# One item of attention taken out of turn, two MLPs stretched, and separate buffers for the last stage of a four-layer kernel

## The reference, cut to what matters

```python
# L0: RMS norm, 8 query heads of 64 on one key head, rotary; gated MLP 512 -> 2048 -> 512
x = x + softmax(rope(q(h)) @ rope(k(h)).T / 8) @ v(h) @ Wo.T        # h = ada_rms(x)
x = x + (silu(h @ Wg.T) * (h @ Wu.T)) @ Wd.T                        # h = ada_rms(x)
# L1: layer norm, 16 heads of 32, unit-length q and k; MLP with tanh gelu
x = x + (softmax(qn @ kn.T + mask) @ v @ Wproj.T + bproj) * gamma1
x = x + (gelu_tanh(h @ Wfc1.T + bfc1) @ Wfc2.T + bfc2) * gamma2
# L2: layer norm, 16 query heads of 32 on 4 key heads through a latent, banded mask; no MLP
x = x + attention(h) @ Wo.T
# L3: 8 experts, each on its own 64 channels, then a norm and a projection
y = gelu(x_e @ W1_e + b1_e) @ W2_e + b2_e                           # exact gelu
x = x + silu(layernorm(y) * (1 + scale) + shift) @ out_W + out_b
```

## Time and profile before

| what | value |
|---|---|
| median of 3 runs | 2262.67 us (2260.27 to 2266.0) |
| profiled execution, its own time | 2263.43 us |
| its span, first to last instruction | 2261.6 us |
| PE busy in the span | 1991.7 us, 88% |
| DVE, ACT, POOL busy | 1139.3, 1033.9, 795.2 us |
| TensorE clock granted, mean | 0.928 |

### The profile page before, as it was taken

The page is one execution under the profiler, slowest core; times in us unless marked ns, Lnnn a source line. Parts: engine busy times, 40 slices in busy tenths (PEclk is TensorE's granted clock), DMA queues, the critical chain, the costliest instruction groups (busy, mean ns, idle before and its releaser), DMA issues. The chain is left out here.

```text
span 2261.6 us, 35138 instructions
## 1 busy us (share of the span) xinstructions
PE 1991.7 (88%) x12920; PEld 1560.5 (69%) x12920; DVE 1139.3 (50%) x3157; ACT 1033.9 (46%) x2445; POOL 795.2 (35%) x1095
## 2 busy tenths in 40 slices
PE   5698999899999999998999899999889975877675
PEld 3476778687778878886778788778767753635353
DVE  3645444643453455346645655565465454544442
ACT  2423322332343344434554565455365467474744
POOL 4454444111124233334656434243233333322210
PEclk9789989999999999999999999999999997987977
DMA  7225566444444544454445343334433520312100
GB/s 269 80 83 177 180 235 236 152 168 149 163 138 160 197 149 142 148 187 145 155 140 196 130 154 128 131 117 140 141 125 131 192 97 29 103 38 83 39 29 19
DMA packets 93659, 309.58 MB, mean 137 GB/s; under 512 B 10417, under 2 KB 11185, under 8 KB 91825
## 3 DMA queue, kind: packets, MB, share of 16 engines
q1 hardware_dynamic: 93488, 307.34, 39.2%
HBM read 240.19 MB, written 67.11 MB: 136 GB/s over the span
## 5 line engine op out<-in xcount | busy, mean ns | idle before, releaser
L164 POOL TENSOR_SCALAR SS<-SS,NM 128x256 f32<-128x256 f32 (+1 forms) x640 | 290.4, 471 | 909.8 <-DVE NM L179 909.8
L149 PE MATMUL B<-HM,W 128*128 128x512 f32 x2496 | 589.4, 396 | 23.6 <-DVE HM L167 15.1
L149 PEld LDWEIGHTS B<-HM,W 128*128 128x128 f32 x2496 | 475.5, 191 | 125.5 <-issue 22.6
L149 PE MATMUL B<-G,W 128*128 128x512 f32 x1536 | 409.8, 418 | 34.7 <-DVE FB L170 17.7
L149 PEld LDWEIGHTS B<-G,W 128*128 128x128 f32 x1536 | 299.3, 199 | 110.2 <-issue 44.0
L155 ACT ACTIVATE SS<-SS,NM 128x256 f32<-128x256 f32 (+1 forms) x512 | 240.6, 471 | 205.9 <-DVE NM L164 205.1
L152 PE MATMUL B<-ident,SS 128*128 128x128 f32 x1152 | 185.2, 301 | 63.2 <-POOL SS L164 52.8
L149 PE MATMUL B<-HA,W 128*128 128x512 f32 x864 | 227.1, 414 | 6.9 <-DVE HA L167 6.3
L152 PEld LDWEIGHTS B<-ident,SS 128*128 128x128 f32 x1152 | 134.2, 150 | 99.7 <-POOL SS L164 58.3
L149 PEld LDWEIGHTS B<-HA,W 128*128 128x128 f32 x864 | 167.2, 200 | 46.4 <-DVE HA L167 6.7
L167 DVE TENSOR_TENSOR G<-FB,G 128x512 fp32r<-128x512 f32 x128 | 102.2, 799 | 160.7 <-ACT G L155 160.7
(11 more groups left out here) (102 smaller groups left out, 2680.6 us busy)
## 6 DMA issues: line engine op xcount, KB each, us to landing
W<-kept SPq DMA_DIRECT2D x360, 512.0 KB, 4.2
kept<-W SPq DMA_DIRECT2D x120, 512.0 KB, 4.7
ST<-in_wpack SPq DMA_DIRECT2D x120, 256.0 KB, 3.0
Y<-in_adaw SPq DMA_DIRECT2D x12, 1024.0 KB, 6.5
out_xT<-X SPq DMA_DIRECT2D x16, 256.0 KB, 2.0
X<-in_xT SPq DMA_DIRECT2D x1, 3072.0 KB, 14.3
FB<-in_pos SPq DMA_DIRECT2D x4, 256.0 KB, 5.0
X<-in_xT SPq DMA_DIRECT2D x1, 1024.0 KB, 6.0
```

What stands on the lines that cost most here:

```text
L149: return self.real.matmul(*a, **k) if self.real is not None else self
L164: return self.real.tensor_scalar(*a, **k) if self.real is not None else self
```

## The change

It has five parts.

1. **The order of the items** becomes a table. The seventh and eighth places are now (layer 2, chunk 0) and (layer 1, chunk 3): item 7 is layer 2 of chunk 0, item 8 is layer 1 of chunk 3, the rest as before. All formulas on g go through it.
2. **The positions** are now a table of numbers, `PLACE`, with a start and an end of its own for each MLP and single positions for norms, projections, experts and last products.
3. **G has memory of its own**, so that the experts no longer wait for the last MLP. W12 and its DMA are gone: the expert weights are four pieces of 128x512 (256 KB) that go through the two stages ST, one per group t and chunk, unsplit.
4. **z writes its high and low parts into the memory of T and Y** (ZH, ZL) in place of HM. The statistics of the next norm, which use T and Y, therefore wait until the four `last` products of the z before them are done.
5. **WSLOTS 11 to 8, FBUFS 5 to 7.**

```diff
-ITEMS = 12
+ORDER = ((0, 0), (0, 1), (0, 2), (0, 3), (1, 0), (1, 1), (1, 2), (2, 0), (1, 3), (2, 1), (2, 2), (2, 3))
...
-PIECES = 120
-WSLOTS = 11
+PIECES = 124
+WSLOTS = 8
...
-FBUFS = 5
+FBUFS = 7
...
-UPS = (20.4, 38.4, 55.8, 71.8, 87.8, 103.8, 119.8, 135.8, 151.8)
+PLACE = {
+    "up": [20.25, 37.774, 53.238, 69.246, 84.763, 103.509, 123.675, 150.322],
+    "up end": [35.49, 53.408, 66.177, 84.262, 100.64, 123.811, 147.706, 164.324],
+    "m norm": [17.582, 34.064, 49.554, 66.056, 81.912, 97.369, 120.398, 147.186],
+    "m final": [19.93, 36.106, 52.069, 68.347, 84.611, 99.748, 122.714, 149.431],
+    "a norm": [3.951, 20.163, 36.916, 52.263, 68.917, 84.642, 101.558, 116.342, 131.609, 150.183, 166.089],
...
+    "first": [137.43, 168.366, 179.31, 201.305],
+    "z norm": [141.577, 174.923, 183.457, 207.201],
+    "z final": [144.398, 176.596, 185.493, 212.617],
+    "last": [145.545, 178.406, 187.993, 221.687],
...
+    "experts": [0.314, 0.533, 1.113, 0.998],
+    "z stats": [-0.298, 0.784, 0.756, 1.406, 2.27],
+    "z parts": [0.874, 2.977, 1.615, 0.743],
+    "last step": [0.67],
...
+    "down": [0.802],
...
-        self.at(UPS[8] + 0.2, self.add, "w12")
...
-        with nc.sbuf_tensor("G", [128, 4, 2, 512], F32R) as G:
-            pass
+        G = sb("G", [128, 4, 2, 512], F32R)
         GF = sb("GF", [128, 4, 512])
-        W12 = sb("W12", [128, 4, 512])
...
+        with nc.sbuf_tensor("ZL", [128, 4, 512], F32R) as ZL:
+            pass
         Y = sb("Y", [128, 4, 512])
...
+        with nc.sbuf_tensor("ZH", [128, 4, 512], F32R) as ZH:
+            pass
         T = sb("T", [128, 4, 512])
...
+        def stats_read(i):
+
+            return p_last.of(i[2], 3) if i[0] == "z" else p_var.of(i)
...
                     e.wait_ge(*source_ready(i))
-                    e.wait_ge(*p_var.of(norm_before[i]))
+                    e.wait_ge(*stats_read(norm_before[i]))
...
-                    w, x = W12[:, t, :], X[:, t, 512 * n:512 * n + 512]
-                    e.wait_ge(*s_w12.of())
+                    w, x = ST[:, weights.stage(number(n, "experts", 3, t)), :], X[:, t, 512 * n:512 * n + 512]
+                    e.wait_ge(*ready(n, "experts", 3, t))
...
-                    product(dp.buf(u)[:, :], [(part(w, 128 * c, 128 * c + 128), (HM[:, 0, c, :], HM[:, 1, c, :]))
+                    product(dp.buf(u)[:, :], [(part(w, 128 * c, 128 * c + 128), target(("z", 0, n), c))
...
-            return p_second.of(*divmod(i - 1, 4)) if i else p_down.of(7, 3, 3)
+            return p_second.of(*divmod(i - 1, 4)) if i else (None, 0)
...
-                elif kind == "w12":
-                    e.wait_ge(*p_down.of(7, 3, 3))
-                    e.dma_start(W12[:, :, :], w12).then_inc(*s_w12.up())
```

More of the change, by code:

```diff
@@ L186, in halves, with layer, _kept_values @@
     return ap.rearrange("p (b s) -> p b s", b=2)
+def layer(g):
+    return ORDER[g // 16][0]
 def unit(g):
-    return g // 64, (g // 16) % 4, (g // 4) % 4, (g // 2) % 2, g % 2
+    return *ORDER[g // 16], (g // 4) % 4, (g // 2) % 2, g % 2
 def keys(g):
-    return 128 if g // 64 == 2 and g % 2 == 0 else 256
+    return 128 if layer(g) == 2 and g % 2 == 0 else 256
+def _kept_values():
+    first, ends = [], []
+    for k, (L, n) in enumerate(ORDER):
+        first.append(len(ends))
+        ends += [16 * k + 4 * t + 3 for t in range(4)] if L == 1 else [16 * k + 15]
+    return first, ends
+KV_FIRST, KV_END = _kept_values()
 def kv_number(L, n, t):
-    return n if L == 0 else 4 + 4 * n + t if L == 1 else 20 + n
+    return KV_FIRST[ITEM[L, n]] + (t if L == 1 else 0)
 def pair(g):
@@ L334, in unit @@
         if 0 <= g < UNITS:
-            us = [self.dp.take() for _ in range(keys(g) * HEADS[g // 64] // 512)]
+            us = [self.dp.take() for _ in range(keys(g) * HEADS[layer(g)] // 512)]
             self.add("turn", g, us)
@@ L493, in pieces_of @@
         return [("down", q // 4, 4 * c + j) for j in range(4)], q % 4
+    if kind in ("first", "second"):
+        return [("experts", 3, a[1])], a[0]
     if kind == "last":
@@ L577, in spread @@
             need = [self.number[name, n] for name in names]
-            while waiting and not (self.raw(waiting[0])):
+            while waiting and not self.raw(waiting[0]):
                 do(waiting.pop(0))
@@ L583, in spread, with program @@
                 assert x < w and x not in waiting, (step, x, w)
+                while self.plain(x) and self.order[x] >= loaded:
+                    load()
             out.append(step)
+            if step[0] == "second":
+                split += 1
+                load()
             store(lambda y: False)
-            if waiting:
+            if waiting and (not self.raw(waiting[0]) or self.order[waiting[0]] < split + STAGES):
                 do(waiting.pop(0))
         return out
-def program(nc, xT, pos, condT, biasd, cols, consts, tab2, wpack, w12, adaw, out):
+def program(nc, xT, pos, condT, biasd, cols, consts, tab2, wpack, adaw, out):
     ctx = ExitStack()
@@ L1014, in tensor @@
                     r.then_inc(*p_second.up(n, t))
+                    w = number(n, "experts", 3, t)
+                    stused[weights.order[w]] = (p_second, (n, t))
                 elif kind == "last":
```

178 lines of the change are left out of this document (103 added, 75 removed), and 1 row of the table PLACE.

## The result

The changed kernel takes **2168.81 us** (median of 4 runs, 2165.85 to 2172.67) where the kernel before, on the same chip, takes 2261.47 (2259.09 to 2266.0): ratio 0.9589, 95% interval 0.9567 to 0.9611, 93 us less. The forecast was 2230 us, 32 less, with 2192 as the low end. The profiled execution took 2169.68 us.

What follows compares the result with a forecast made beforehand. PE bounds the kernel (busy 1991.7 of 2261.6 us), so reordering wins only its standing and low clock. 2263.4 - 43 + 8 + 3 + 2 - 3 = 2230.4, put at 2230 us; own range 2216 to 2244, with rivals 2192 to 2262.

Steps and rivals of the forecast that it cites:

- The cover: Units 152 to 164: MLP 7 replaces the chunk 0 tail's thin chain there; gain 43 us, ends 39 and 47.
- The 6.6 us: Loss left for the 76.0 us of work of units 152 to 164 once covered, at 8.7%.
- MLP 7's share: Units 152 to 164: some 75 us of MLP put there, 12 of 14 units.
- The gaps: 10.8 units without an MLP, attention alone: 8 us lost at 0.75 a unit, from 0 to 17.
- Eight places: Weight fetches at part starts begin later with 8 places, not 11; few land late: 3 us lost.
- the third rival: Slower: at 32 part starts PE waits for fetches landing in 8 us, 80 us for 3; 2307 us, chance 0.12.
- z in T and Y: After chunk 0's tail, MLP 7's norm wants T before the last product is done; 2 us lost, once.
- The start: Before unit 20: slices called a thin start; no term for it in the sum.
- The spacing of the tails: Tails of chunks 1 to 3: z statistics further apart, later z norm in chunk 1; 3 us gained, from 0 to 27.
- None is on the path: 0 us: Chunk 0 tail's new place: twelve more ACT table loads, 15 us of ACT, priced at 0 us.
- The rival of more: Last 300 us: half the T and gelu waits freed, 19 us, 27 with the clock; 2204 us, chance 0.20.

## Why the prediction was right in direction and wrong in size

**The cover, 43 us: right in the sum, not place by place.** Unit 152 to 164 takes 120.8 us (forecast 120 to 130) with PE at 98% and a clock of 0.99. The stretch lost 49.6 us and loses 120.8 - 117.6 = 3.2. Unit 152 comes 57.5 us earlier, of which 17.3 lie before unit 20 and 40.2 behind it, where the forecast had 40. But the tail of chunk 0 now lies in units 136 to 151, and these lose 27.5 us where they lost 4.1 in the kernel before; units 128 to 135 lose 1.0 for 18.2. With the natural order units 136 to 151 lose 133.6 - 0.92 x 119.0 = 24.1 us with no tail in them, so the 27.5 aren't the tail's alone. The 6.6 us that the prediction left for the covered work can be read off no stretch. Nor can the term be read off one experiment, since undoing the stretch of MLPs 5 and 6 keeps MLP 7's and gives 18 us. (MLP 7's share in that paragraph, 12 of 14 units, is 80 us and not 75; the sum doesn't use it.)

**The gaps, +8 us: wrong in sign.** Closing three of the gaps makes the kernel 24 us slower. The step that failed was to take two rows of the end of layer 2, and "lost a unit" from them, for what attention alone would do behind an MLP of layers 0 and 1. It charged the gap for itself and nothing for the parts, the norm and the output product that crowd together without it. Which of these it is, no run shows.

**Eight places, +3 us: about right here, by the wrong wait.** At the old positions they cost some 12 us in units 16 to 79, 9.9 of them in PE's waits for POOL's split of a new piece; at the new ones eight against nine cost nothing visible. No fetch is waited for, so the third rival (2307 us) is out, and its 8 us of landing never came up: the median is 4.3.

**z in T and Y, +2 us.** It wasn't tried by itself. The wait where it was put is small: in units 136 to 151 of the changed kernel PE stands for T 4.9 us in two waits, with and without cover much the same.

The stretch from 20 to 163 is 45.0 us shorter, not 30. That is 15 of the 61 us missed.

**The start, no term: 17 us.** The step that failed is the list of what moves: it had the MLPs, the tails and the buffers, and treated the new positions of the first item (q, k, v, norm, trig) as nothing, after calling the start thin. The earlier trace rows had the sign of it, PE at 5 and 6 tenths and then the clock at 7. The runs put 12 us of it on the positions (7 on the value product alone) and 5 to 6 on the smaller pool.

**The spacing of the tails, -3 us: 31.6, with 29 back in one run.** This is the step that failed by most. The prediction had the wait (27.2 us for T) and even its full size as an end, and then took a tenth of it. It also had the rival: half of the waits for T and gelu, 19 us, with the clock that comes back, 27 us. The size and the place are that rival's, the make-up only in part: T and gelu fell by 13 us, and the waits for PT and CX, which no term priced, by 10. From unit 164 on, the spacing of z's steps is 14.9 us of it and the later starts, above all of chunk 1, are 16.4; the prediction named both, the spacing and that start (174.6 for 172.3), and put them at 3 us together. Over the whole kernel close statistics cost 10.4 us and parts not kept together 14.8, and these don't add; the prediction had no price for the parts.

"None is on the path: 0 us" was said of table loads in the tail of chunk 0. In units 136 to 151, where that tail now lies, PE stands for the gelu 2.7 us. It said nothing of the uncovered tails, where one order of z and softmax on ACT and DVE costs 15 us more than another. The figure of the Trainium skill, "ScalarE: Activation LUTs", What ACT_TABLE_LOAD costs, of 2.66 us a switch is not what this case shows, as the prediction already had it from the earlier trace rows: the next operation starts 1.29 us after the load does (2070.60 to 2071.89). By it the four loads of the spread parts would be an estimated 10.6 us, by the rows they are 5.1.

The likelihoods follow. The rival of more (2204 us) was right about the end; no case had the start, and none had a gap that pays. Of the 35 us by which that rival is too high, these two (17 us, and 8 charged for gaps) are 25. It counts its 27 us on top of the 3 that are in the sum; in place of them it would be 2206.

## What to carry to other kernels

Where one merged list drives every engine, price each position that moves, the first ones too, and ask of each chain without cover in what order its steps reach the engines that feed it: when a late norm starts, how far apart its steps stand and whether its parts come in one block was worth as much here (31.6 us) as three quarters of what the cover was put at. Where the clock is below 1.0, spacing can win more than the idle time that it removes: from unit 164 on PE stands 22 us less and the stretch is 31.6 shorter. A reordering and the room that it needs can be separated by putting back the order alone; here the order was worth no more than the 5 us between two overlapping intervals. And two edits that make a third are not proven to be its halves by medians that add up: lay the lengths of the stretches side by side.

## What the runs showed of the hardware that was not expected

A quarter of a unit in the position of one kind of product cost 8.5 us, more than the first of them itself (5.84 us). The same 48 matmuls of 128x128 by 64 took 9.58 us at a granted clock of 0.55, right behind waits of 1.96 and 0.81 us, and 5.84 us at 1.00, with no wait right before them.

Less cover cost clock as well as waiting: from unit 164 on, the stretch of before lost 128.7 us at a granted clock of 0.82, and the one after loses 273.8 - 0.87 x 206.24 = 94.4 us at 0.87. PE is busy for 206.24 us instead of 215.45, with the same work in it to a few microseconds.

A larger pool was slower: eleven places (and five FB) took 6 us more than ten (and seven FB) in the kernel before, most of it ahead of unit 0 (63.1 us for 58.4), where a split that waits 5.84 us for its data stands in front of what the first unit needs.
